# A vision tower with a mixture of experts on one core: the small steps of the attention stage in a new order

## The chip, the core and the metric

The kernel runs on one core of a Trainium2 chip. The core has TensorE (PE in the profile, with PEld for its weight loads), VectorE (DVE), ScalarE (ACT), GpSimd (POOL) and SyncE (SP, which here only issues DMAs). Each engine takes its own instructions strictly in the order in which they are written, and engines wait for each other with semaphores. The metric is the time of one execution on the device in microseconds (us).

## What is computed

16 images of 1024 patches, embedded in 64 dimensions; then an attention layer with 8 heads of 8 dimensions and a bias by column; then a mixture of 8 experts of which each token takes 2.

```python
h = tok(x)                                   # patches @ W + b + pos_embed
h = h + attn(layernorm(h), ...)
h = h + ffn(layernorm(h), ...)

# attn
q, k, v = (x @ W + b).reshape(B, N, H, hd)   # for q, k and v
scores = einsum('bihd,bjhd->bhij', q, k) / sqrt(hd) + col_bias
out = einsum('bhij,bjhd->bihd', softmax(scores), v) @ Wo + bo

# ffn
probs = softmax(tokens @ router_w.T)
rw, re = top_k(probs, 2); rw = rw / max(rw.sum(-1), 1e-12)
out = tokens
for e in range(8):
    h = gelu(tokens @ w1[e] + b1[e])
    out = out + combine[:, e] * (h @ w2[e] + b2[e])
```

## The kernel before

After a short first part (constants, the column bias, the preparation of the first images) the kernel has two stages: attention over the 16 images one after the other, and the experts over 64 units, four per image. The change touches the attention stage alone.

One image of attention is 32 **quads** (`QUADS`). A quad is two **blocks**, each a tile of 128x1024 scores in one of three PSUM buffers (`SCORE_BUFS`). In quad q TensorE issues four matmuls of scores (L1448, bf16), then a small step if one has its place there, then the eight passes of values of quad q - 2 (L1464, probabilities times v, accumulated in `o_acc` over eight quads). ScalarE takes the exp of each block (L1246), 64 per image. The scores of a block wait for the exp that last used its buffer; the values wait for the exps of their quad.

The small steps serve the neighbouring images. While image b is in attention, steps for the next image b + 1 run (`PREP`: qk0 and qk1 make the two halves of q and k, v makes v, sq the squares from which a bound on the scores comes), the embedding and normalisation of b + 2 (`LEAD`: embed, norm_t), and what follows attention for b - 1 (`POST`: out_proj, post_t, router, combine_t). `AUX_SLOTS` is a table written by hand: quad number to step and half. All steps share one PSUM bank, `aux`. A step waits (`aux_drained`) until VectorE has read what the step before left there, and VectorE waits (`aux_filled`) for the matmuls.

VectorE runs through the same 32 slots. A slot is only an order there: VectorE goes on as soon as its waits allow. In each slot it first does the evacuation that is due (`evacuate`, L1314 to L1319, slots 9, 17, 25, and 1 of the next image: it transposes `o_acc` out of PSUM and divides by the sum; the next values that write `o_acc` wait for its first instruction), then scale_tokens, shift_of and flag_of, lead_centre or normalise if the slot is theirs, then the drain of the step that ended in this quad, then centre_tokens, ranking (rank_experts, order_experts) or weigh_experts. The drain of qk1 is followed by `split_high` and `split_low`, which cut q and k into bf16 parts; SyncE stores these parts and loads them back as QA and KA for the next image, behind block 32 for the first half of the heads. `shift_of` needs a square root that GpSimd makes from the result of sq (L387). The exps of the router run on ScalarE behind block `ROUTER_EXP_BLOCK`. At slots 0 and 16 stands a fallback for large scores, whose branch isn't taken here, but for which TensorE waits until ScalarE has come to block 0 or 32.

Names in the rows: L481 is the drain of qk0 and qk1, L495 the reduction of sq, L563 and L565 scale_tokens, L575 the drain of out_proj, L581 of post_t, L584 and L585 of router, L597 to L615 ranking, L621 to L635 weigh_experts, L456 the drain of embed, L430 with `centred` lead_centre, L468 normalise, L486 the drain of v, L591 of combine_t. On TensorE L662 is qk, L686 out_proj, L681 sq, L672 post_t, L691 router, L650 embed, L666 v, L696 combine_t, L656 norm_t.

Of the kernel before, what the change touches and what calls it, by code (L numbers as in the profile page):

```python
# [12 lines left out]
NB = 16  # L13
# [33 lines left out]
EVAC_SLOTS = {8 * g + 7 + LAG: g for g in range(3)}  # L47
LAST_EVAC_SLOT = LAG - 1

AUX_SLOTS = {0: ("qk0", 0), 2: ("qk0", 1), 4: ("qk1", 0), 6: ("qk1", 1), 8: ("out_proj", 0), 10: ("out_proj", 1),  # L50
             12: ("sq", 0), 14: ("post_t", 0), 16: ("router", 0), 18: ("router", 1), 20: ("embed", 0),
             22: ("embed", 1), 24: ("v", 0), 26: ("v", 1), 28: ("combine_t", 0), 30: ("norm_t", 0)}
HALVED = ["qk0", "qk1", "out_proj", "router", "v", "embed"]
LEAD = ["embed", "norm_t"]
PREP = ["qk0", "qk1", "v", "sq"]
POST = ["out_proj", "post_t", "router", "combine_t"]
FIRST_STEPS = ["embed_0", "embed_1", "norm_t_0", "qk0", "qk1", "v", "sq", "norm_t_1"]
FIRST_DRAINS = ["embed_0", "embed_1", "qk0", "qk1", "v", "sq", "norm_t_1"]
CENTRE_SLOT, SCALE_SLOT, SHIFT_SLOT, LEAD_SLOT, NORM_SLOT = 10, 12, 14, 23, 26
ROUTER_EXP_BLOCK = 40  # L60
BUF_TURN = 38

PAIRS = NX // 2
# [5 lines left out]
CENTRE_UNIT, SCALE_UNIT = 4, 5  # L69
ROUTER_UNIT = 15  # L70
RANK_UNIT, ORDER_UNIT, WEIGH_UNIT = 16, 17, 18
COMBINE_SLOT, WEIGH_SLOT = 20, 25
Y_BUFS = 2
H_BUFS = 4
RQ_LIMIT, RQ_CLIP = 31.0, 32.0
# [15 lines left out]
def step_of(b, slot):  # L91

    if slot not in AUX_SLOTS:
        return None
    step, part = AUX_SLOTS[slot]
    image = b + (2 if step in LEAD else 1 if step in PREP else -1)
# [3 lines left out]
def is_last(step, part):  # L100
    return part == 1 or step not in HALVED
# [11 lines left out]
def aux_count(b, step):  # L113
    return aux_before(b) + aux_order(b).index(step) + 1
# [7 lines left out]
def attention(nc, pool, io, psum, scratch, out):  # L122
# [4 lines left out]
    with ctx:  # L127
# [173 lines left out]
        def later(b):  # L301

            return not (isinstance(b, int) and b == 0)

        def by_half(rows):
            return rows.rearrange("p (t c) d -> p t c d", t=2)

        def by_chunk(bank):
            return bank.rearrange("p (c t e) -> p t c e", t=2, e=D)

        def alone(eng):

            eng.sem_inc(stood_alone, 1)
# [88 lines left out]
        def vector_steps(v):  # L402

            def chain(sem, base, total):

                count = [0]

                def link(ins):
                    count[0] += 1
                    ins.then_inc(sem, 1)  # L410
                    v.wait_ge(sem, base + count[0])

                def close():
                    assert count[0] == total, (count[0], total)
                return link, close
# [55 lines left out]
            def prep_step(step, bp, filled, st, bank=aux, full=aux_filled, free=aux_drained, freed=None):  # L471

                freed = freed or filled
                if step == "qk0":
                    st["link"], st["close"] = chain(prep_chain, PREP_CHAIN * bp, PREP_CHAIN)
                link, close = st["link"], st["close"]
                if full is not None:
                    v.wait_ge(full, filled)
                if step in ("qk0", "qk1"):
                    n = int(step[-1])  # L480
                    v.tensor_scalar(qk[:, n * BANK:(n + 1) * BANK], bank, b_qk[:, 0:1], scale_qk[:, 0:1],  # L481
                                    ALU.add, ALU.mult).then_inc(free, 1)
                if step == "v":
                    if later(bp):
                        v.wait_ge(va_ready, 2 * bp)
                    v.tensor_tensor(by_half(v_new[:, :, :]), by_chunk(bank),  # L486
                                    b_v[:, :].unsqueeze(1).unsqueeze(1).broadcast_to([P, 2, NCH // 2, D]),
                                    ALU.add).then_inc(free, 1)
                elif step == "qk1":
                    v.wait_ge(free, freed)  # L490
                    split_high(bp, link)
                    if bp:
                        split_low(link)
                elif step == "sq":
                    v.reduce_max(sq_max[:, :], bank, AX.X).then_inc(free, 1)  # L495
                    v.wait_ge(free, freed)
                    alone(v)
                    square_bounds(link)
# [18 lines left out]
            def split_high(bp, link):  # L517
                if bp == 1:
                    v.wait_ge(first_stored[1], PARTS_STORES // 2)
                if bp > 1:  # L520
                    v.wait_ge(parts_stored, PARTS_STORES * (bp - 1))
                link(v.tensor_copy(qk_parts[:, 0, :], qk[:, :]))
                if bp:
                    link(v.tensor_tensor(qk_rest[:, :], qk[:, :], qk_parts[:, 0, :], ALU.subtract))
                v.tensor_tensor(squares[:, :], qk_parts[:, 0, :], qk_parts[:, 0, :],
                                ALU.mult).then_inc(squares_ready, 1)
                if not bp:
                    link(v.tensor_tensor(qk_rest[:, :], qk[:, :], qk_parts[:, 0, :], ALU.subtract))

            def split_low(link):  # L530
                link(v.tensor_copy(qk_parts[:, 1, :], qk_rest[:, :]))
                v.tensor_tensor(qk_parts[:, 2, :], qk_rest[:, :], qk_parts[:, 1, :],
                                ALU.subtract).then_inc(parts_ready, 1)

            def square_bounds(link):
                v.tensor_copy(sq_moved[:, 0:1], sq_max[SECOND:SECOND + H, :])
                v.tensor_copy(sq_moved[:, 1:2], sq_max[32:32 + H, :])
                link(v.tensor_copy(sq_moved[:, 2:3], sq_max[32 + SECOND:32 + SECOND + H, :]))
                v.tensor_tensor(q_sq_max[:, :], sq_max[0:H, :], sq_moved[:, 0:1], ALU.max)
                link(v.tensor_tensor(k_sq_max[:, :], sq_moved[:, 1:2], sq_moved[:, 2:3], ALU.max))  # L540
                v.tensor_tensor(rq2[:, :], q_sq_max[:, :], k_sq_max[:, :], ALU.mult).then_inc(rq2_ready, 1)
# [560 lines left out]
        with nc.Block() as block:  # L1102
# [136 lines left out]
            def _(act):  # L1239
# [27 lines left out]
                def body(b):  # L1267
                    act.wait_ge(flag_ready, b + 1)
                    flag = act.value_load(flags[0:1, ds(b, 1)], min_val=0, max_val=1)
                    for k in range(BLOCKS):  # L1270
                        if k % (BLOCKS // 2) == 0:
                            fallback(b, k // (BLOCKS // 2), flag)
                        exp_block(b, k)
                        if k == ROUTER_EXP_BLOCK and b:
                            router_exp(aux_count(b, "router"))
# [24 lines left out]

            @block.vector
            def _(v):
                chain, _, _, (lead_step, lead_centre, normalise), prep_step, (shift_of, flag_of), _ = vector_steps(v)
                post_step, centre_tokens, scale_tokens, rank_experts, order_experts, weigh_experts = vector_post(v)

                def evacuate(b, g):
# [46 lines left out]
                def body(b):  # L1353
                    v.wait_ge(flag_ready, b + 1)
                    flag = v.value_load(flags[0:1, ds(b, 1)], min_val=0, max_val=1)
                    st = {}
                    for slot in range(QUADS):
                        if slot % 16 == 0:
                            fallback(b, slot // 16, flag)
                        if slot in EVAC_SLOTS:  # L1360
                            evacuate(b, EVAC_SLOTS[slot])
                        if slot == SCALE_SLOT and b:
                            scale_tokens(b - 1, st)
                        if slot == SHIFT_SLOT and b + 1 < NB:
                            shift_of(b + 1, st)
                            flag_of(b + 1, st)
                        if slot == LEAD_SLOT and b + 2 < NB:
                            lead_centre(b + 2, st)
                        if slot == NORM_SLOT and b + 2 < NB:
                            normalise(b + 2)  # L1370
                        found = step_of(b, slot)
                        if found and is_last(found[0], found[1]):
                            step, _, image = found
                            if step in LEAD:
                                lead_step(step, image, aux_count(b, step), st)
                            elif step in PREP:
                                prep_step(step, image, aux_count(b, step), st)
                            else:
                                post_step(step, image, aux_count(b, step), st)
                        if slot == LAST_EVAC_SLOT and b:  # L1380
                            evacuate(b - 1, 3)
                        if slot == CENTRE_SLOT and b:
                            centre_tokens(b - 1, st)
                        if slot == COMBINE_SLOT and b:
                            rank_experts(b - 1, st)
                            order_experts(b - 1, st)
                        if slot == WEIGH_SLOT and b:
                            weigh_experts(b - 1, st)
# [18 lines left out]
                st = {}  # L1407
# [246 lines left out]
```

## Time and profile before

| | us |
|---|---|
| runs of the kernel | 1175.14, 1176.40, 1176.45 (median 1176.4) |
| profiled execution, its own time | 1174.37 |
| its span, first to last instruction | 1172.4 |
| TensorE busy | 1093.3 (93%) |
| ScalarE busy | 1029.6 (88%) |
| VectorE busy | 612.0 (52%) |
| GpSimd busy | 126.6 (11%) |

The granted clock of TensorE is 0.985 of full speed over the span and full from the second image of attention on. The first exp of attention starts at 47.6 us and the last at 1009.0; the rest is the experts. Busy shares are means over both stages. A row of the timeline gives the start, the duration, the engine and the line; "x4" means four instructions merged into one row, and the part in brackets is idle time of that engine ahead of it with the instruction that ended it. The start of a quad on TensorE is the start of the "x4" row of L1448.

### The profile page before, as it was taken

The page shows a single profiled execution, that of the slowest core. Times are in us where ns is not written, and L with a number is a line of the kernel's source. Part 1 is how long each engine was busy: PE and PEld are TensorE (multiplying, and loading weights), DVE is VectorE, ACT ScalarE, POOL GpSimd, SP SyncE. Part 2 cuts the span into 40 slices and gives each one's busy share as a digit, 9 for nine tenths or more (in the row PEclk, how much of TensorE's full clock was granted, in tenths as well). Part 3 has the DMA queues.
Part 4 walks back from the last instruction along what each step waited for, and adds up shares of the span by engine and source line. Part 5 has one row for each costly group of instructions (what it writes and reads, how often), then busy time and mean ns, then how long its engine had stood idle before and what let it go on. Part 6 is the DMA issues. An engine that isn't in the chain of part 4 may idle for free. (4 is left out here: it accounts for less than half of the span.)

```text
span 1172.4 us, 21673 instructions
## 1 busy us (share of the span) xinstructions
PE 1093.3 (93%) x7913; PEld 318.5 (27%) x7914; DVE 612.0 (52%) x1700; ACT 1029.6 (88%) x1127; POOL 126.6 (11%) x137
## 2 busy tenths in 40 slices
PE   3599999999999999999999999999999999899998
PEld 2122222222222222222222222222222222233332
DVE  8433555554545454555545454545454424467665
ACT  1399999999999999999999999999999999754553
POOL 3204010101001010101111110101010000000000
PEclk7699999999999999999999999999999999999999
DMA  2531313131222122323231322223131320022321
GB/s 53 123 84 41 92 42 92 43 89 43 82 46 73 49 76 51 83 51 83 52 83 47 87 48 61 74 56 78 40 86 33 92 61 10 14 61 71 84 73 50
DMA packets 62128, 75.06 MB, mean 64 GB/s; under 512 B 26220, under 2 KB 30572, under 8 KB 61996
## 3 DMA queue, kind: packets, MB, share of 16 engines
q1 hardware_dynamic: 59740, 73.03, 24.1%
q8 instruction: 79, 1.29, 0.5%
q14 instruction: 53, 0.43, 0.1%
q10 hardware_dynamic: 1776, 0.24, 0.1%
q0 software_dynamic: 480, 0.06, 0.1%
HBM read 36.70 MB, written 35.65 MB: 62 GB/s over the span
## 5 line engine op out<-in xcount | busy, mean ns | idle before, releaser
L1246 ACT ACTIVATE probs<-psum 128x1024 f32<-128x1024 f32 x1024 | 944.3, 1138 | 42.5 <-PE psum L1448 42.5
L1464 PE MATMUL psum<-probs,VA 128*32 128x512 f32 x4096 | 545.7, 605 | 1.1 <-ACT probs L1246 0.5
L1448 PE MATMUL psum<-QA,KA 54*128 54x512 bf16 x2048 | 326.2, 384 | 10.2 <-issue 3.1
L1448 PEld LDWEIGHTS psum<-QA,KA 54*128 54x128 bf16 x2048 | 74.4, 93 | 471.9 <-ACT probs L1246 436.9
L1314 DVE STREAM_TRANSPOSE oT<-psum 128x512 f32<-128x512 f32 x64 | 45.9, 717 | 218.6 <-PE psum L1464 218.6
L1464 PEld LDWEIGHTS psum<-probs,VA 128*32 128x32 f32 x4096 | 82.5, 108 | 147.5 <-issue 114.8
L1281 ACT ACTIVATE probs<-psum,b 128x1024 f32<-128x1024 f32 x64 | 67.8, 1110 | 53.4 <-PE psum L1517 53.4
L1395 DVE TENSOR_TENSOR probs<-probs,psum 128x1024 f32<-128x1024 f32 x64 | 78.2, 1221 | 51.3 <-PE psum L1527 31.1
L481 DVE TENSOR_SCALAR qk<-psum,b_qk,scale_qk 128x512 f32<-128x512 f32 x32 | 25.3, 793 | 85.3 <-PE psum L662 85.3
L1185 POOL TENSOR_TENSOR p_rstd<-p_ve,neg_half 128x8 f32<-128x8 f32 x16 | 32.3, 2021 | 310.5 <-DVE p_ve L427 310.5
L1517 PE MATMUL psum<-m_x,w 64*128 64x512 f32 x256 | 60.5, 591 | 1.5 <-ACT probs L1281 1.5
L1541 PE MATMUL psum<-probs,w 128*64 128x512 f32 x256 | 60.9, 598 | 0.0
L383 POOL TENSOR_TENSOR rstd<-ve,neg_half 128x8 f32<-128x8 f32 x16 | 31.5, 1970 | 266.5 <-DVE ve L427 266.5
L662 PE MATMUL psum<-xnT,w_qk 64*128 64x256 f32 x128 | 38.1, 398 | 0.8 <-ACT xnT L842 0.8
L392 POOL COPY VA<-v_new 128x256 f32<-128x256 f32 x32 | 12.7, 398 | 235.0 <-PE psum L1464 136.1
L462 DVE COPY xnT<-psum 128x512 f32<-128x512 f32 x15 | 10.4, 691 | 47.5 <-PE psum L656 47.5
L597 DVE TENSOR_REDUCE r_sum<-router_e 128x8 f32<-128x64 f32 x16 | 3.5, 220 | 54.0 <-ACT router_e L1251 54.0
L650 PE MATMUL psum<-w_tok,xT 128*128 128x128 f32 x128 | 23.2, 308 | 8.3 <-DMA tok_b<-in_tok_b 6.9
L1527 PE MATMUL psum<-m_cT,spread 64*128 64x512 bf16 x128 | 24.6, 382 | 6.2 <-DVE probs L1395 6.2
L1517 PEld LDWEIGHTS psum<-m_x,w 64*128 64x128 f32 x256 | 24.3, 188 | 19.3 <-issue 15.2
L1288 ACT ACTIVATE yT<-psum 128x512 f32<-128x512 f32 x16 | 9.6, 597 | 20.1 <-PE psum L1541 20.1
L1319 DVE TENSOR_TENSOR oT_norm<-oT,o_inv 128x128 f32<-128x128 f32 x64 | 24.7, 386 | 2.3
(171 smaller groups left out, 778.6 us busy)
## 6 DMA issues: line engine op xcount, KB each, us to landing
QA<-q_parts_d SPq DMA_DIRECT2D x64, 192.0 KB
KA<-k_parts_d SPq DMA_DIRECT2D x64, 192.0 KB
q_parts_d<-qk_parts SPq DMA_DIRECT2D x32, 192.0 KB, 2.4
k_parts_d<-qk_parts SPq DMA_DIRECT2D x32, 192.0 KB, 2.7
xT<-in_xT SPq DMA_DIRECT2D x16, 256.0 KB, 2.6
q_parts_d<-qk_parts SPq DMA_DIRECT2D x32, 128.0 KB, 2.6
k_parts_d<-qk_parts SPq DMA_DIRECT2D x32, 128.0 KB, 2.5
x_d<-x2T SPq DMA_DIRECT2D x16, 256.0 KB, 2.1
```

The source lines that it names most:

```text
L383: g.tensor_tensor(rstd[:, :], ve[:, :], neg_half[:, :], ALU.pow).then_inc(rstd_ready, 1)
L481: v.tensor_scalar(qk[:, n * BANK:(n + 1) * BANK], bank, b_qk[:, 0:1], scale_qk[:, 0:1], ALU.add, ALU.mult).then_inc(free, 1)
L662: last = pe.matmul(aux[:, cols], w_qk[rows, :, :].rearrange("k a e -> k (a e)"), xnT[rows, cols], start=True, stop=True)
L1185: g.tensor_tensor(p_rstd[:, :], p_ve[:, :], neg_half[:, :], ALU.pow).then_inc(p_rstd_ready, 1)
L1246: nc.scalar.activation(probs[:, k % PROB_BUFS, :], score_buf(buf_of(k)), ACT.Exp).then_inc(exped, 1)
L1281: nc.scalar.activation(act_h[:, u % H_BUFS, :], hid[u % 2], ACT.Gelu, bias=b1[:, u % PAIRS:u % PAIRS + 1]).then_inc(gelued, 1)
L1314: v.transpose(oT[:, :, :].rearrange("p j r -> p (j r)"), o_acc).then_inc(o_evacuated, 1)
L1395: v.tensor_tensor(gated[:, u % H_BUFS, :], act_h[:, u % H_BUFS, :], wgt, ALU.mult).then_inc(gated_ready, 1)
L1448: last = pe.matmul(score_buf(buf_of(k))[:, (g % 2) * BANK:(g % 2 + 1) * BANK], KA[rows_of(h, SCORE_ROWS), h // 2, jt * P:(jt + 1) * P], QA ...
L1464: last = pe.matmul(o_acc[32 * g:32 * g + 32, :], VA[:, jt, h, :], probs[:, k % PROB_BUFS, (g % 2) * BANK:(g % 2 + 1) * BANK], start=(jt == ...
L1517: last = pe.matmul(hid[u % 2][:, t * BANK:(t + 1) * BANK], w1[rows, m, :], m_x2[rows, b % 2, :], start=True, stop=True)
L1541: last = pe.matmul(ysum[D * t:D * (t + 1), :], w2[:, m, :], gated[:, u % H_BUFS, t * BANK:(t + 1) * BANK], start=False, stop=(m == PAIRS - 1))
```

## The change

`AUX_SLOTS` gets another order: out_proj goes from quads 8 and 10 to 4 and 6, qk1 from 4 and 6 to 8 and 10, post_t (the transposes of x) from 14 to 12, the router's halves from 16 and 18 to 14 and 16, sq from 12 to 18, the first half of embed from 20 to 19; all others keep their quads. On VectorE centre_tokens goes to slot 6, scale_tokens to 10, split_low gets a slot of its own (13), shift_of and flag_of go to 20, ranking to 19, weigh_experts to 22, normalise to 28. The router's exp on ScalarE goes from behind block 40 to behind block 36. No instruction is added or taken away.

```diff
...
-AUX_SLOTS = {0: ("qk0", 0), 2: ("qk0", 1), 4: ("qk1", 0), 6: ("qk1", 1), 8: ("out_proj", 0), 10: ("out_proj", 1),
...
+AUX_SLOTS = {0: ("qk0", 0), 2: ("qk0", 1), 4: ("out_proj", 0), 6: ("out_proj", 1), 8: ("qk1", 0), 10: ("qk1", 1),
...
-CENTRE_SLOT, SCALE_SLOT, SHIFT_SLOT, LEAD_SLOT, NORM_SLOT = 10, 12, 14, 23, 26
-ROUTER_EXP_BLOCK = 40
+CENTRE_SLOT, SCALE_SLOT, SPLIT_SLOT, SHIFT_SLOT, LEAD_SLOT, NORM_SLOT = 6, 10, 13, 20, 23, 28
+ROUTER_EXP_BLOCK = 36
...
-COMBINE_SLOT, WEIGH_SLOT = 20, 25
+COMBINE_SLOT, WEIGH_SLOT = 19, 22
...
                     split_high(bp, link)
-                    if bp:
-                        split_low(link)
...
+                        if slot == SPLIT_SLOT and b + 1 < NB:
+                            split_low(st["link"])
```

What stands in a row on each engine, at the places where the work moves. In these lines the operands stand behind the arrow, and line numbers of the changed kernel differ by one or two.

TensorE before, quads 12 to 14 of an image: sq, and two quads later the transposes of x.

```order
L1448 MATMUL psum<-QA,KA 128x512 x4
L681 MATMUL psum<-squares,sel_sq 32x512 x4
L1464 MATMUL psum<-probs,VA 32x512 x4
L1448 MATMUL psum<-QA,KA 128x512 x4
L1464 MATMUL psum<-probs,VA 32x512 x4
L1448 MATMUL psum<-QA,KA 128x512 x4
L672 MATMUL psum<-ident,x 128x128 x4
L1464 MATMUL psum<-probs,VA 32x512 x4
```

TensorE now, quads 10 to 12: the transposes of x come behind the second half of qk1.

```order
L1449 MATMUL psum<-QA,KA 128x512 x4
L660 MATMUL psum<-xnT,w_qk 128x256
L1465 MATMUL psum<-probs,VA 32x512 x4
L1449 MATMUL psum<-QA,KA 128x512 x4
L1465 MATMUL psum<-probs,VA 32x512 x4
L1449 MATMUL psum<-QA,KA 128x512 x4
L670 MATMUL psum<-ident,x 128x128 x4
L1465 MATMUL psum<-probs,VA 32x512 x4
```

TensorE now, quads 18 and 19: sq comes right ahead of the first half of embed, in neighbouring quads.

```order
L1449 MATMUL psum<-QA,KA 128x512 x4
L679 MATMUL psum<-squares,sel_sq 32x512 x4
L1465 MATMUL psum<-probs,VA 32x512 x4
L1449 MATMUL psum<-QA,KA 128x512 x4
L648 MATMUL psum<-w_tok,xT 128x128 x2
L1465 MATMUL psum<-probs,VA 32x512 x4
```

VectorE before, slots 12 to 14: scale_tokens, the reduction of sq, its bounds, shift and flags, and then the drain of the transposes of x.

```order
L563 TENSOR_TENSOR x<-p_centred,p_rstd 128x2x4x64
L565 TENSOR_TENSOR H_all<-h,x 128x512
L495 TENSOR_REDUCE sq_max<-psum 128x1
L536 COPY sq_moved<-sq_max 8x1
...
L541 TENSOR_TENSOR rq<-q_sq_max,k_sq_max 8x1
L506 TENSOR_SCALAR shift_row<-minus_ones,rq 8x1024
...
L514 TENSOR_SCALAR flags<-rq_top 1x1
L581 COPY x2T<-psum 128x512
```

VectorE now, slots 16 to 20: the evacuation stands ahead of the reduction of sq, and the ranking between its bounds and the shift.

```order
L583 TENSOR_TENSOR logits<-psum,logit_max 128x64
L1313 STREAM_TRANSPOSE oT<-psum 128x512
L1316 RECIPROCAL o_inv<-oT 128x16
L1318 TENSOR_TENSOR oT_norm<-oT,o_inv 128x16x8
L493 TENSOR_REDUCE sq_max<-psum 128x1
L534 COPY sq_moved<-sq_max 8x1
...
L595 TENSOR_REDUCE r_sum<-router_e 128x8
...
L613 TENSOR_REDUCE rank<-above 128x64
L504 TENSOR_SCALAR shift_row<-minus_ones,rq 8x1024
...
L512 TENSOR_SCALAR flags<-rq_top 1x1
```

VectorE before, slots 23 to 28: weigh_experts and normalise stand between the evacuation and the drain of v.

```order
L430 TENSOR_TENSOR centred<-H_all,mv 128x512
L1314 STREAM_TRANSPOSE oT<-psum 128x512
L1317 RECIPROCAL o_inv<-oT 128x16
L1319 TENSOR_TENSOR oT_norm<-oT,o_inv 128x16x8
L621 SCALAR_TENSOR_TENSOR chosen<-rank,rprob 128x64
...
L635 COPY comb_parts<-comb_parts 128x8x24
L468 TENSOR_TENSOR xn<-centred,rstd 128x2x4x64
L486 TENSOR_TENSOR v_new<-psum,b_v 128x512
L591 COPY cT<-psum 128x512
```

VectorE now, slots 22 to 28: weigh_experts stands ahead of lead_centre and the evacuation, and the drain of v right behind them, ahead of normalise.

```order
L456 TENSOR_TENSOR H_all<-psum,posb 128x512
L419 BN_STATS stats<-H_all 128x6 x8
L619 SCALAR_TENSOR_TENSOR chosen<-rank,rprob 128x64
...
L633 COPY comb_parts<-comb_parts 128x8x24
L425 BN_AGGR mv<-stats 128x2 x8
L427 TENSOR_SCALAR ve<-mv 128x8
L430 TENSOR_TENSOR centred<-H_all,mv 128x512
L1313 STREAM_TRANSPOSE oT<-psum 128x512
...
L1318 TENSOR_TENSOR oT_norm<-oT,o_inv 128x16x8
L486 TENSOR_TENSOR v_new<-psum,b_v 128x512
L468 TENSOR_TENSOR xn<-centred,rstd 128x2x4x64
L589 COPY cT<-psum 128x512
```

## Rows read from the trace of the kernel before

**Rows 1.** One line, ScalarE's exp: count, duration ns min/median/max, first and last start.
```profile
L1246 ACT ACTIVATE probs<-psum x1024: 1017/1124/1582, 47.6 to 1009.0; 128x1024 f32<-128x1024 f32 x171
```

**Rows 2.** ScalarE timeline, one image; columns: start, duration, engine, line, tiles, count, idle before.
```profile
497.99 10.19 ACT L1246 ACTIVATE probs<-psum 128x1024 f32<-128x1024 f32 x11 [0.55 <-PE psum L1448]
...
508.10 15.82 ACT L1246 ACTIVATE probs<-psum 128x1024 f32<-128x1024 f32 x17
...
524.65 33.10 ACT L1246 ACTIVATE probs<-psum 128x1024 f32<-128x1024 f32 x36 [0.73 <-PE psum L1448]
558.30 10.19 ACT L1246 ACTIVATE probs<-psum 128x1024 f32<-128x1024 f32 x11 [0.55 <-PE psum L1448]
```

**Rows 3.** Who waited for whom, whole span; columns: total us, times, longest.
```profile
PE psum L672 <- DVE sq_max L495: 12.4, 14, 1.0
...
PE psum L696 <- DVE v_new L486: 14.0, 14, 1.0
...
PEld psum L1448 <- ACTq L1265: 26.0, 31, 0.8
```

**Rows 4.** Timeline around the first stall, quads 14 and 15, PE and DVE.
```profile
493.84 0.69 DVE L563 TENSOR_TENSOR x<-p_centred,p_rstd 128x512 f32<-128x512 f32 x1 [1.61 <-POOL p_rstd L1185]
...
494.24 0.91 PE L1448 MATMUL psum<-QA,KA 54*128 54x512 bf16 x4
...
495.18 0.68 DVE L495 TENSOR_REDUCE sq_max<-psum 128x1 f32<-128x512 f32 x1
...
496.01 0.63 PE L672 MATMUL psum<-ident,x 128*128 128x128 f32 x4 [0.86 <-DVE sq_max L495]
...
497.56 0.61 PE L1448 MATMUL psum<-QA,KA 54*128 54x512 bf16 x4
...
497.69 0.47 DVE L506 TENSOR_SCALAR shift_row<-minus_ones,rq 8x1024 bf16<-8x1024 bf16 x1 [0.80 <-POOL rq L387]
...
498.58 0.69 DVE L581 COPY x2T<-psum 128x512 f32<-128x512 f32 x1
```

**Rows 5.** Timeline around the second stall, quads 26 to 30, DVE and PE.
```profile
517.77 0.72 DVE L1314 STREAM_TRANSPOSE oT<-psum 128x512 f32<-128x512 f32 x1 [1.64 <-PE psum L1464]
...
519.14 0.22 DVE L621 SCALAR_TENSOR_TENSOR chosen<-rank,rprob 128x64 f32<-128x64 f32 x1
...
521.24 0.61 PE L1448 MATMUL psum<-QA,KA 54*128 54x512 bf16 x4
...
521.55 0.68 DVE L468 TENSOR_TENSOR xn<-centred,rstd 128x512 f32<-128x512 f32 x1
522.15 0.68 DVE L486 TENSOR_TENSOR v_new<-psum,b_v 128x512 f32<-128x512 f32 x1
...
522.89 0.40 PE L696 MATMUL psum<-ident_bf,comb_parts 128*128 128x128 bf16 x4 [1.04 <-DVE v_new L486]
...
524.22 0.60 PE L1448 MATMUL psum<-QA,KA 54*128 54x512 bf16 x4
...
525.75 0.61 PE L1448 MATMUL psum<-QA,KA 54*128 54x512 bf16 x4
```

**Rows 6.** Timeline, steps that the change moves, DVE and PE, same image.
```profile
472.59 0.60 PE L1448 MATMUL psum<-QA,KA 54*128 54x512 bf16 x4
...
474.62 0.61 PE L1448 MATMUL psum<-QA,KA 54*128 54x512 bf16 x4
...
480.95 0.81 DVE L481 TENSOR_SCALAR qk<-psum,b_qk,scale_qk 128x512 f32<-128x512 f32 x1 [4.86 <-PE psum L662]
...
508.35 0.22 DVE L597 TENSOR_REDUCE r_sum<-router_e 128x8 f32<-128x64 f32 x1 [3.59 <-ACT router_e L1251]
...
510.11 0.61 PE L1448 MATMUL psum<-QA,KA 54*128 54x512 bf16 x4
...
512.29 0.61 PE L1448 MATMUL psum<-QA,KA 54*128 54x512 bf16 x4
...
515.45 0.69 DVE L430 TENSOR_TENSOR centred<-H_all,mv 128x512 f32<-128x512 f32 x1
```

More of the change, by code:

```diff
@@ L48 @@
 LAST_EVAC_SLOT = LAG - 1
-AUX_SLOTS = {0: ("qk0", 0), 2: ("qk0", 1), 4: ("qk1", 0), 6: ("qk1", 1), 8: ("out_proj", 0), 10: ("out_proj", 1),
-             12: ("sq", 0), 14: ("post_t", 0), 16: ("router", 0), 18: ("router", 1), 20: ("embed", 0),
-             22: ("embed", 1), 24: ("v", 0), 26: ("v", 1), 28: ("combine_t", 0), 30: ("norm_t", 0)}
+AUX_SLOTS = {0: ("qk0", 0), 2: ("qk0", 1), 4: ("out_proj", 0), 6: ("out_proj", 1), 8: ("qk1", 0), 10: ("qk1", 1),
+             12: ("post_t", 0), 14: ("router", 0), 16: ("router", 1), 18: ("sq", 0), 19: ("embed", 0), 22: ("embed", 1),
+             24: ("v", 0), 26: ("v", 1), 28: ("combine_t", 0), 30: ("norm_t", 0)}
 HALVED = ["qk0", "qk1", "out_proj", "router", "v", "embed"]
@@ L1302, in _ @@
             def _(v):
-                chain, _, _, (lead_step, lead_centre, normalise), prep_step, (shift_of, flag_of), _ = vector_steps(v)
+                chain, _, _, (lead_step, lead_centre, normalise), prep_step, (shift_of, flag_of), rest = vector_steps(v)
+                split_low = rest[2]
                 post_step, centre_tokens, scale_tokens, rank_experts, order_experts, weigh_experts = vector_post(v)
```

## The prediction, made before the changed kernel was run

> **What bounds the kernel now.** The page's busy shares, which I read first, do not decide it: TensorE and ScalarE both look nearly full, over two stages of different kinds. So I read ScalarE's own timeline over one image of the attention stage. ScalarE runs 64 exps of 128x1024 per image. One stretch of 36 of them takes 33.10 us from first start to last end, and the shortest of all exps is 1.02 us, so one exp costs (33.10 - 1.02) / 35 = **0.917 us** when nothing is late [rows 1, 2]. 64 of them are 58.67 us. The image's period is 558.30 - 497.99 = 60.31 us [rows 2]. Of the 1.64 us between them, about 0.16 is the small exp of the router, which sits before 508.10: the 17 exps behind it need 15.59 and end at 523.92, 15.74 after the end of the 11 exps before it. The other **1.48 us** are two idle times with "PE psum L1448" as releaser: 0.55 us ahead of block 30 and 0.73 us ahead of block 58 [rows 2]. Since neighbouring exps overlap by 1.02 - 0.92 = 0.10 us, each costs 0.10 more than its idle time: 0.65 and 0.83.
>
> So ScalarE bounds the attention stage, except in two places per image where the scores of TensorE come late. Who made them late? Two waits stand out by their counts: TensorE's transposes of x (L672) waited for sq_max on VectorE 14 times, 12.4 us in all, and its transposes of the expert weights (L696) for v_new 14 times, 14.0 us in all, at most 1.0 us each [rows 3]. Fourteen is the number of images that have both a next image to prepare and one before to finish (images 1 to 14).
>
> In rows 4 to 6 one reads "quad starts" (the x4 rows of L1448). At the first stall quad 14 starts at 494.24, VectorE reduces sq only at 495.18 to 495.86, because scale_tokens stood before it, and the transposes, which write the same PSUM bank, start at 496.01, having waited 0.86. Quad 15 begins at 497.56 instead of about 1.2 earlier, and block 30's exp follows 0.43 after that [rows 2, 4]. At the second, weigh_experts starts at 519.14, xn at 521.55 and v_new at 522.15, so the aux bank is free only at 522.83, while quad 28 had begun at 521.24; the wait is 1.04 and quad 29 starts at 524.22, 0.43 before block 58's exp [rows 2, 5].
>
> **How much room TensorE has.** A quad without a small step lasts 525.75 - 524.22 = 1.53 us [rows 5], one with half of embed 512.29 - 510.11 = 2.18 [rows 6], one with half of qk0 and an evacuation by VectorE, which the values must await, 474.62 - 472.59 = 2.03 [rows 6], the combine transposes without their wait 524.22 - 521.24 - 1.04 = 1.94 [rows 5]. ScalarE takes 2 x 0.917 = 1.83 per quad. I call lead the time by which a quad starts before it would delay an exp; that point is 0.43 + 0.10 = 0.53 before the end of the exp ahead. A quad without a step adds 0.30 to the lead, one with a step takes 0.11 (combine), 0.20 (qk) or at most 0.35 (all other). Check on before: the second stall. The 17 exps end at 508.10 + 15.82 = 523.92, less 0.53 is 523.39, quad 29 starts at 524.22: lead -0.83, which is the loss read above. The whole of TensorE's image is 60.31 less the two waits with what they made wait, 0.86 + 1.04, so at most 58.4, below ScalarE's 58.83: with the waits gone ScalarE can set the pace, with little to spare.
>
> **The change, part by part.**
>
> Step 1: out_proj goes to quads 4 and 6, qk1 to 8 and 10. All counts stay. out_proj needs qk0's drain and the last evacuation of the image before, both queued at quad 2. That evacuation takes 519.14 - 517.77 = 1.37 [rows 5], plus a transpose of about 0.7, then the drain of 0.81 [rows 6], together 3.0 from 0.2 into quad 2; out_proj is due 2.03 + 1.53 + 0.54 = 4.1 into it (0.54 being the scores ahead of a step). Hidden, cover 0.9.
>
> Step 2: the transposes of x (post_t) go to quad 12, behind qk1 instead of sq. VectorE from 0.2 into quad 10: evacuation 1.37, scale_tokens 495.18 - 493.84 = 1.34 or a little more [rows 4], qk1's drain 0.81, and about 0.12 to TensorE: bank free 3.9 into quad 10. TensorE arrives at 2.03 + 1.53 + 0.54 = 4.1. The wait of 0.86 goes, cover 0.2. This frees **0.65 us**.
>
> Step 3: split_low (some 1.9 us, two of VectorE's 128x1024 operations) moves behind the drain of post_t, to slot 13. Its 12 stores on SP start some 7 quads later; behind them on SP stand the store of x2, the loads of QA and KA for the next image, which wait for block 32 anyway, and the row of shifts, which is now made at slot 20. The next image starts 12 quads, 22 us, after that slot, and a chain of some 20 issues fits in; then come the load of x, wanted in the next image's quad 19, and the store of the combine weights. Cost nothing; if the stores took over 20 us more, the next image would start late. The router's halves at 14 and 16 wait for x2T, which comes after split_high, about 3 us behind the qk1 drain; quad 14's step is due 3.7 after quad 12's. Cost nothing.
>
> Step 4: sq goes to quad 18. VectorE is then at the evacuation of slot 17 for 1.37 from 0.2 into the quad, reduces sq in 0.68 and frees the bank 2.4 into it. The first half of embed now stands in quad 19 and is due 2.03 + 0.54 = 2.57 into quad 18. Cover 0.2: the **tightest place**. If gone, each 0.1 beyond the lead costs 0.1 per image. Quad 18 itself grows: sq alone would be under 2.03, but the evacuation holds the values; I take 2.03.
>
> Step 5: ranking (slot 19), shift (20), embed and weighing (22), then lead_centre (23), then the evacuation of slot 25, due 0.2 into quad 26. On VectorE, from 1.6 into quad 18: the sq reduction and bounds, shift and flags are 498.58 - 495.18 = 3.40, less the 0.80 wait for POOL that ranking now covers, 2.6 [rows 4]; ranking, embed and centring 516.14 - 508.35 = 7.8 [rows 6]; weighing 521.55 - 519.14 = 2.4 [rows 5]. It ends 14.5 after quad 18's start. Quad 26 starts 8 quads after, 8 x 1.83 + 0.14 = 14.8, and its evacuation is due at 15.0. Cover about 0.5. Behind it v is drained and xn made, before quad 28's transposes are due 3.7 + 0.5 after quad 26. The wait of 1.04 goes: **0.83 us**.
>
> Leads in the new order. After quad 16, TensorE cannot start before ScalarE has come to block 32 (the ACTq row, 31 times) [rows 3]; before, the lead there was 0.30 (zero after the stall, one free quad). From 0.30 at quad 0: 0.10 after it, then 0.20, 0.15, 0.10, 0.20, 0.30, 0.25, 0.20 after quads 2 to 14. From 0.30 at 16: -0.05 at 17, 0.30 at 18, with the router's exp 0.24 at 19, -0.11 at 20; then 0.60 at 22, 0.25, 0.20, 0.15 after 22, 24, 26, and 0.3 at the end. So the worst is 0.16 per image. But ScalarE's starts run ahead of its ends when it is not made to wait, and then quad 16 may start with 0.5, and nothing is lost. The bounds are 0 and 0.16 x 14 = 2.2 us; I take 0, as no stall resets ScalarE at quad 15.
>
> **Sum.** 14 x (0.65 + 0.83) = 20.7 us. The first image, the last one and the feed-forward stage keep their order of costs. The profiled execution took 1174.4 us and becomes 1153.7; the runs' median is 1176.4, 2.0 above it, and becomes **1155.7**.
>
> **A rule that speaks against it.** The trace gives 0.917 per exp over 36 in a row, and 1.02 for the shortest alone [rows 1, 2]. The Trainium skill, "ScalarE: Activation LUTs", section "What ACT_TABLE_LOAD costs", gives 186 ns plus 0.833 ns per element, with back-to-back activations overlapping by about 93 ns: an estimate of 946 ns for 1024. By it ScalarE would need 60.5 + 0.16 us per image, more than the measured period, and there would be nothing to win: 1176. The trace disagrees by 0.03 per exp.
>
> **Rivals.**
> (a) Forecast: both stalls vanish, 1153 to 1158.
> (b) One cover is gone. At quad 19 or before the evacuation of quad 26 VectorE is late by 0.3 to 0.8 us more than I count, and the lead of 0.1 to 0.5 swallows part. Loss 0.2 to 0.7 per image, 3 to 10 us: 1158 to 1166. For it: covers of 0.2 in steps 2 and 4. Against: durations on VectorE repeat from image to image.
> (c) No gain: ScalarE is saturated in a way that gives the idle back, for instance each exp stretched to 0.94 once it is fed without pause. 64 x 0.94 = 60.2, or 1.4 more than ScalarE needs here, which eats the 1.48: about 1175. This is where the rule above would lead. Against: 36 exps in a row run at 0.917 [rows 2].
> (d) Slower: VectorE's unbroken run of 13 us between quads 18 and 26. If ranking can't start when sq is done, because the router's exp comes after block 36 and is itself late, everything to the evacuation slides. From 0.5 + 0.5 us of slide TensorE's values wait and ScalarE stalls; from 2.5 us it costs more than the 1.48 gained. At 3.5 us it is 1.0 x 14 = +14, so 1190. Against: the logits are made 2 quads ahead of block 36, as before they were of block 40.
>
> **Chances.** (a) 0.74, (b) 0.16, (c) 0.04, (d) 0.06. A measurement tells about 0.2%, 2.4 us, from no change: faster 0.90, same 0.04, slower 0.06. The range holds (a) with its 2.2 us and the runs' own 1.3 us of spread, and the larger part of (b): 1152.5 to 1163.
>
> **What would show it.** Right: the waits of L670 (transposes of x) for sq_max and of the combine transposes for v_new are gone; ScalarE's timeline has no idle in an image, and the period is 58.8 us. Step 4 wrong: embed's matmuls wait for sq_max in quad 19. Step 5 wrong: values in quad 26 wait for oT's transpose. Step 2 wrong: the transposes of x wait for qk. Rival (c): exps of over 0.92 us without idle between them.

## The result and the profile after

| | before | after |
|---|---|---|
| median of the runs | 1175.77 us | 1154.60 us (1154.36 to 1155.46) |
| ratio after to before | | 0.9823, 95% interval 0.9806 to 0.9840 |
| span of the profiled execution | 1172.4 us | 1152.3 us |

The change makes the kernel 21 us faster, against 1155.7 us predicted. The profiled execution took 1154.4, against 1153.7 predicted. With the same two views as in [rows 2, 3], ScalarE's timeline of the changed kernel (start, duration, line, tiles, count) reads:

```profile
469.00 26.12 ACT L1244 ACTIVATE probs<-psum 128x1024 f32<-128x1024 f32 x28
494.70 0.55 ACT L1249 ACTIVATE router_e<-logits 128x64 f32<-128x64 f32 x1
494.85 59.08 ACT L1244 ACTIVATE probs<-psum 128x1024 f32<-128x1024 f32 x64
553.50 0.55 ACT L1249 ACTIVATE router_e<-logits 128x64 f32<-128x64 f32 x1
```

There is no idle time left in brackets. 64 exps go from 494.85 to the next router exp without one, and the period is 553.50 - 494.70 = 58.80 us, where [rows 2] had 60.31. 13 of the 14 full images had two stalls, image 14 one and a small one. From the starts of the exps in the two traces: images 1 to 14 took 843.9 us before and 823.2 after, 20.8 less; the first image 0.4 less, the last 0.2 more, the time ahead of the first exp 0.7 more. From the start of the last exp to the end it is 163.3 before and 163.5 after. With this the parts add up to the difference of the spans, 20.0. The 0.7 ahead of the first exp is no effect of the change: that exp starts anywhere between 47.5 and 48.5 us in the runs below.

The page's groups for ScalarE's exp, before and after (line, tiles, count, busy us, mean ns, idle before it, releaser):

```profile
L1246 ACT ACTIVATE probs<-psum 128x1024 f32<-128x1024 f32 x1024 | 944.3, 1138 | 42.5 <-PE psum L1448 42.5
```

```profile
L1244 ACT ACTIVATE probs<-psum 128x1024 f32<-128x1024 f32 x1024 | 940.9, 1249 | 25.7 <-PE psum L1449 25.7
```

Of this idle time 23.8 and 24.5 us lie ahead of the very first exp (the longest single wait in the list of waits), so inside the stage it falls from 18.7 to 1.2 (the 1.2 is one wait in the first image, which both kernels have). With the 0.10 us of overlap that each of the 27 stalls also destroys, these are 20.2 of the 20.8 us. The mean duration rises from 1138 to 1249 ns although each exp costs the same, 0.917 us between ends. I read this as waiting behind the exp ahead that is recorded inside the duration. Durations of single exps say nothing here; distances between ends do.

Now the covers of the critical steps, that is the time between VectorE's release of what TensorE waits for and TensorE's use of it. Quad 12, the transposes of x behind the drain of qk1 (before: [rows 4]):

```profile
481.31 0.80 DVE L481 TENSOR_SCALAR qk<-psum,b_qk,scale_qk 128x512 f32<-128x512 f32 x1
...
482.02 0.72 PE L1449 MATMUL psum<-QA,KA 54*128 54x512 bf16 x4
...
482.66 0.66 PE L670 MATMUL psum<-ident,x 128*128 128x128 f32 x4
```

The bank is free at 482.11 and used at 482.66, with no wait. Behind the first stall stood one more wait, which the prediction shows in its rows and does not reason with. In [rows 4] VectorE sat idle for 1.61 us before scale_tokens, until GpSimd had made `p_rstd` from the result of centre_tokens. The lists of waits, before and after:

```profile
DVE x L563 <- POOL p_rstd L1185: 24.4, 16, 1.6
```

```profile
DVE x L561 <- POOL p_rstd L1183: 0.3, 1, 0.3
```

Before, two slots lay between the two steps, and TensorE waited 0.86 us behind them; now there are four, and GpSimd's result is there in time. Without the 1.61 us the reduction of sq would have ended at about 494.25, ahead of the transposes, which were due at 495.15. So this idle time alone accounts for the first stall. No run moves scale_tokens by itself, so that is worked out and not shown. Quads 18 and 19, sq and embed:

```profile
493.08 0.66 PE L1449 MATMUL psum<-QA,KA 54*128 54x512 bf16 x4
...
494.65 0.68 DVE L493 TENSOR_REDUCE sq_max<-psum 128x1 f32<-128x512 f32 x1
...
495.18 0.61 PE L1449 MATMUL psum<-QA,KA 54*128 54x512 bf16 x4
...
495.71 0.71 PE L648 MATMUL psum<-w_tok,xT 128*128 128x128 f32 x4
```

sq is read by 495.33, embed's matmuls come 0.53 into quad 19, where they are due, at 495.71: 0.38 later. Quads 26 and 28 (before: [rows 5]):

```profile
508.01 0.61 PE L1449 MATMUL psum<-QA,KA 54*128 54x512 bf16 x4
508.25 0.72 DVE L1313 STREAM_TRANSPOSE oT<-psum 128x512 f32<-128x512 f32 x1 [0.42 <-PE psum L1465]
...
509.62 0.68 DVE L486 TENSOR_TENSOR v_new<-psum,b_v 128x512 f32<-128x512 f32 x1
...
512.26 0.40 PE L694 MATMUL psum<-ident_bf,comb_parts 128*128 128x128 bf16 x4
```

VectorE is idle for 0.42 us before the evacuation of quad 26, so its long run (from the reduction of sq on, see step 5 of the prediction) ended that much before its time, and v is drained at 510.30, 2 us before the transposes of the expert weights.

### The profile page after: what moved, and what is told of

The parts are those of the page before. It is cut to its first block and busy times, and to the rows that moved or that the text cites. A ratio compares the mean times of both kernels' runs of the same rounds, so it can differ in the third digit from the quotient of the medians.

```text
span 1152.3 us, 21645 instructions
## 1 busy us (share of the span) xinstructions
PE 1100.7 (96%) x7913; PEld 326.2 (28%) x7914; DVE 610.2 (53%) x1700; ACT 1026.2 (89%) x1127; POOL 130.2 (11%) x137
## 5 line engine op out<-in xcount | busy, mean ns | idle before, releaser
L1244 ACT ACTIVATE probs<-psum 128x1024 f32<-128x1024 f32 x1024 | 940.9, 1249 | 25.7 <-PE psum L1449 25.7
L1449 PE MATMUL psum<-QA,KA 54*128 54x512 bf16 x2048 | 331.8, 385 | 8.4 <-issue 3.6
L1449 PEld LDWEIGHTS psum<-QA,KA 54*128 54x128 bf16 x2048 | 82.2, 93 | 484.5 <-ACT probs L1244 446.5
L573 DVE TENSOR_TENSOR h<-psum,H_all 128x512 f32<-128x512 f32 x16 | 11.1, 692 | 80.9 <-PE psum L684 80.9
L387 POOL TENSOR_TENSOR rq<-rq,half 8x1 f32<-8x1 f32 x16 | 8.7, 546 | 307.1 <-DVE rq L539 307.1
L392 POOL COPY VA<-v_new 128x256 f32<-128x256 f32 x32 | 16.4, 513 | 194.1 <-PE psum L1465 175.5
L582 DVE TENSOR_REDUCE logit_max<-psum 128x8 f32<-128x64 f32 x16 | 3.6, 224 | 53.6 <-PE psum L689 53.6
L1518 PEld LDWEIGHTS psum<-m_x,w 64*128 64x128 f32 x256 | 24.3, 188 | 19.2 <-issue 15.2
```

Source lines behind the costliest of these rows:

```text
L1244: nc.scalar.activation(probs[:, k % PROB_BUFS, :], score_buf(buf_of(k)), ACT.Exp).then_inc(exped, 1)
L1449: last = pe.matmul(score_buf(buf_of(k))[:, (g % 2) * BANK:(g % 2 + 1) * BANK], KA[rows_of(h, SCORE_ROWS), h // 2, jt * P:(jt + 1) * P], QA ...
L1518: last = pe.matmul(hid[u % 2][:, t * BANK:(t + 1) * BANK], w1[rows, m, :], m_x2[rows, b % 2, :], start=True, stop=True)
```

## The experiments

All times below are medians of four runs or more; the kernel before had medians of 1175.1 to 1175.4 beside them, and the ratios are to it. "Lead" is used as in the prediction. It was computed in each trace from the end of the exp ahead and the start of the quad.

**1. The first half of the change alone.** weigh_experts and normalise go back to their slots.

```diff
-CENTRE_SLOT, SCALE_SLOT, SPLIT_SLOT, SHIFT_SLOT, LEAD_SLOT, NORM_SLOT = 6, 10, 13, 20, 23, 28
+CENTRE_SLOT, SCALE_SLOT, SPLIT_SLOT, SHIFT_SLOT, LEAD_SLOT, NORM_SLOT = 6, 10, 13, 20, 23, 26
-COMBINE_SLOT, WEIGH_SLOT = 19, 22
+COMBINE_SLOT, WEIGH_SLOT = 19, 25
```

> The changed kernel with weigh_experts back at slot 25 and normalise back at 26, all else as changed (the first half of the change alone). Theory (VectorE's order makes the aux bank late for the transposes of combine): v's drain ends 3.0 us later than now (weighing 2.4, xn 0.6), the transposes in quad 28 wait 1.1 us; the lead of TensorE there is 0.41 us, so the loss is 0.73 per image, 9.7 us over 14 images: 1164 us, with one idle time of ScalarE per image, ahead of block 58, and none ahead of block 30. Rival (the quads of TensorE's steps alone made the gain): no change, 1154.6.

Measured 1164.16 us, ratio 0.9909 (0.9892 to 0.9925). ScalarE's timeline:

```profile
498.77 19.66 ACT L1244 ACTIVATE probs<-psum 128x1024 f32<-128x1024 f32 x21
519.05 39.52 ACT L1244 ACTIVATE probs<-psum 128x1024 f32<-128x1024 f32 x43 [0.63 <-PE psum L1449]
```

One stall per image, 21 exps after the router's (block 58), of 0.63 + 0.10 = 0.73 us, as expected to the hundredth; the lead at quad 29 is -0.73. So the first half removes the first stall and 11 us, and the second half is worth the other 9.6. Apart from split_low (experiment 4) the parts of the first half were not run one by one.

**2. The second half alone, in the kernel before.**

```diff
-CENTRE_SLOT, SCALE_SLOT, SHIFT_SLOT, LEAD_SLOT, NORM_SLOT = 10, 12, 14, 23, 26
+CENTRE_SLOT, SCALE_SLOT, SHIFT_SLOT, LEAD_SLOT, NORM_SLOT = 10, 12, 14, 23, 28
-COMBINE_SLOT, WEIGH_SLOT = 20, 25
+COMBINE_SLOT, WEIGH_SLOT = 20, 22
```

> The kernel before with weigh_experts at slot 22 and normalise at 28 (the second half of the change alone). Theory: the wait of 1.04 us for v_new goes, but ranking still ends as late as before, so weighing pushes the evacuation of slot 25 0.8 us past its time and the values of quad 26 wait 0.67; TensorE has no lead there (-0.01), so ScalarE loses 0.68 in quad 27 instead of 0.84 in quad 29: 1174, 2 us under before. The releaser of the new wait is VectorE's transpose of oT. Rival (each half is worth its own stall): 11 us under before, 1165.

Measured 1174.59 us, ratio 0.9993 (0.9983 to 1.0002): nothing that can be told from no change. The timeline of quad 26, VectorE, TensorE and ScalarE:

```profile
518.51 0.61 PE L1448 MATMUL psum<-QA,KA 54*128 54x512 bf16 x4
...
518.85 0.68 DVE L430 TENSOR_TENSOR centred<-H_all,mv 128x512 f32<-128x512 f32 x1
...
519.57 0.72 DVE L1314 STREAM_TRANSPOSE oT<-psum 128x512 f32<-128x512 f32 x1
...
520.43 1.07 PE L1464 MATMUL psum<-probs,VA 128*32 128x512 f32 x8 [0.67 <-ACT probs L1246]
...
521.86 2.85 ACT L1246 ACTIVATE probs<-psum 128x1024 f32<-128x1024 f32 x3 [0.65 <-PE psum L1448]
```

The transpose of the evacuation, due 0.24 into the quad at 518.75, starts at 519.57 behind lead_centre, and the values wait 0.67. The row names ScalarE as releaser, but the two exps of quad 24, which these values read, had ended by 517.55; the values start 0.14 after the transpose's end at 520.29. The stall moves from block 58 to block 54 and keeps most of its size (0.65 + 0.10 against 0.83). Together the two parts of the second half need the first half, which ends ranking earlier; experiment 3 takes them apart.

**3. Only normalise later, in the kernel before.** NORM_SLOT 26 becomes 28.

> The kernel before with normalise at slot 28 instead of 26, one constant. Theory: v's drain comes 0.6 us earlier, the wait for v_new falls from 1.04 to 0.44 us and the loss from 0.84 to 0.24 per image: 0.6 x 13 = 7.8 us under before, 1168. Rival (the stall at block 58 is made by the length of the transposes or the late weighing, not by the bank): no change, 1176.

Measured 1167.59 us, ratio 0.9936 (0.9920 to 0.9953): 7.6 us for one constant. The waits of TensorE's transposes, in the kernel of this run:

```profile
PE psum L672 <- DVE sq_max L495: 12.4, 14, 1.0
...
PE psum L696 <- DVE v_new L486: 6.2, 14, 0.4
```

The wait for v_new falls from 14.0 us in all [rows 3] to 6.2, the one for sq_max stays, and the loss at quad 29 falls from 0.84 to 0.24. This shows the bank as the cause of the second stall: the length of the transposes was not touched. It also says what failed in experiment 2: normalise alone wins 7.6 us in the old kernel, and weighing earlier on top of it loses 7.0 of them again (1174.59 against 1167.59).

**4. split_low back behind split_high.**

```diff
-                        if slot == SPLIT_SLOT and b + 1 < NB:
-                            split_low(st["link"])
...
                                 prep_step(step, image, aux_count(b, step), st)
+                                if slot == SPLIT_SLOT:
+                                    split_low(st["link"])
```

with SPLIT_SLOT at 10, the slot of qk1's drain.

> The changed kernel with split_low back right behind split_high, in slot 10, ahead of the drain of post_t. Theory: the drain of post_t ends 1.95 us later; it has 0.8 us to spare now, so the router's matmuls in quad 14 wait 1.15 us; the lead there is 0.56 and the step takes 0.25, so 0.85 to 0.95 us lost per image, 12 to 13 us: 1167. Rival (a slot of its own for split_low does nothing, since it is the same work on the same engine): 1154.6.

Measured 1165.55 us, ratio 0.9920 (0.9903 to 0.9936).

```profile
490.63 0.62 PE L1449 MATMUL psum<-QA,KA 54*128 54x512 bf16 x4
491.46 0.68 DVE L579 COPY x2T<-psum 128x512 f32<-128x512 f32 x1
...
492.19 0.52 PEld L689 LDWEIGHTS psum<-w_router,x2T 128*128 128x128 f32 x4 [1.25 <-DVE x2T L579]
492.20 0.62 PE L689 MATMUL psum<-w_router,x2T 128*128 128x16 f32 x4 [0.95 <-DVE x2T L579]
...
493.74 0.60 PE L1449 MATMUL psum<-QA,KA 54*128 54x512 bf16 x4
...
494.17 1.02 ACT L1244 ACTIVATE probs<-psum 128x1024 f32<-128x1024 f32 x1 [0.62 <-PE psum L1449]
```

The router's matmuls, due at 491.2, start at 492.20, 1.0 late instead of the 1.15 expected, and 0.73 plus a later 0.05 is lost per image. That is 11 us, where 12 to 13 were expected. Half of what the change gains depends on the one line that splits split_low off.

**5. ScalarE lighter.** All exps but the first eight take 992 of 1024 columns.

```diff
-                    nc.scalar.activation(probs[:, k % PROB_BUFS, :], score_buf(buf_of(k)),
+                    w = 2 * BANK if b == 0 and k < PROB_BUFS else 2 * BANK - 32
+                    nc.scalar.activation(probs[:, k % PROB_BUFS, 0:w], score_buf(buf_of(k))[:, 0:w],
```

> The changed kernel with the exps over 992 of the 1024 columns (all but the first eight of the first image); the last 32 columns of each block keep old values, so part of the softmax is left out. Theory (ScalarE bounds each image at 58.80 us, TensorE needs 58.0): an exp falls by 0.027 us to 0.890, 64 by 1.7, and TensorE takes over: a period of 58.0 to 58.4, 6 to 12 us less, 1143 to 1149. Rival 1 (TensorE bounds already): no change, 1154.6. Rival 2 (TensorE has much room): 1.7 x 16 = 27 less, 1127.

Measured 1139.38 us, ratio 0.9691 (0.9675 to 0.9708), below the expected range of 1143 to 1149. Its timeline:

```profile
488.43 0.27 ACT L1250 ACTIVATE router_e<-logits 128x64 f32<-128x64 f32 x1
488.58 2.79 ACT L1245 ACTIVATE probs<-psum 128x992 f32<-128x992 f32 x3
491.53 54.99 ACT L1245 ACTIVATE probs<-psum 128x992 f32<-128x992 f32 x61 [0.16 <-PE psum L1450]
546.39 0.27 ACT L1250 ACTIVATE router_e<-logits 128x64 f32<-128x64 f32 x1
```

The period is 546.39 - 488.43 = 57.96. Between the ends of exps that nothing delays the trace has 0.890, so ScalarE needs 64 x 0.890 + 0.13 = 57.09, and the other 0.87 per image are stalls again, many and small. So TensorE bounds here, at 57.96: its quads follow each other at the durations given in the prediction, 1.53 us without a step. The expected period was right at its lower end (58.0); the time was missed since I counted 14 images alike, while ScalarE is lighter in all 16. By the starts of the exps images 1 to 14 gain 12.3 us (0.84 each, more in image 14), the first image 0.9 and the last 1.7; the spans differ by 14.8 and the medians by 15.2.

**6. TensorE lighter.** Half of out_proj is left out in all images but one.

```diff
                     pe.wait_ge(on_ready, GROUPS * (n + 1))
+                    if n and part == 0:
+                        chunks = []
                     for c in chunks:
```

> The changed kernel without the two matmuls of out_proj's first half in all images but one; half of h1 is then made of what the bank held, so that part of the result is left out. TensorE has 0.64 us less in quad 4 of each image. Theory (ScalarE bounds): no change, period 58.80, 1154.6. Rival (TensorE bounds): 0.64 x 14 = 9 less, 1145.6.

Measured 1154.62 us, ratio 0.9819 (0.9803 to 0.9836), against 1154.60. TensorE's 0.64 us per image are worth nothing: ScalarE sets the pace of the changed kernel.

**7. weigh_experts alone back at slot 25.**

> The changed kernel with weigh_experts alone back at slot 25; normalise stays at 28. Theory: v's drain is 2.4 us later, the transposes of quad 28 wait 0.51 us, the lead of 0.41 with 0.03 taken by the step leaves -0.13: 0.13 x 14 = 1.8 us more, 1156.4, at the edge of what can be measured, but the period in the trace is 58.93 against 58.80. Rival (a wait costs its whole length): 0.5 x 14 = 7 more, 1161.7.

Measured 1156.24 us, ratio 0.9835 (0.9818 to 0.9851). The period in the trace is 58.93, the lead at quad 29 -0.13. By the medians alone 1.6 us could not be told from nothing; the trace confirms the expectation. A wait of TensorE of about 0.5 us costs 0.13, because the lead pays for the rest.

**8. The tightest place, measured.** sq is read twice, the first time into a scratch column.

```diff
+                    if bp:
+                        v.reduce_max(fb_max[:, 0:1], bank, AX.X)
                     v.reduce_max(sq_max[:, :], bank, AX.X).then_inc(free, 1)
```

> The changed kernel with one more reduction of the same sq bank (0.68 us, into a scratch column) ahead of the real one, in slot 18. It measures the cover of the tightest place. Theory: the drain of sq ends 0.73 us later, it has 0.26 to spare, so the first half of embed in quad 19 waits 0.47; the lead after quad 19 is 0.12, so 0.35 per image is lost, 14 x 0.35 = 5: 1159.5. Rival 1 (VectorE is off the path): no change. Rival 2 (the delay runs on to the evacuation of quad 26 too): 0.73 x 14 = 10 more, 1165.

Measured 1156.17 us, ratio 0.9835 (0.9819 to 0.9852), a period of 58.96 and 0.16 lost per image, not the 0.35 expected.

```profile
494.93 0.68 DVE L494 TENSOR_REDUCE fb_max<-psum 128x1 f32<-128x512 f32 x1
...
495.46 0.60 PE L1451 MATMUL psum<-QA,KA 54*128 54x512 bf16 x4
495.53 0.68 DVE L495 TENSOR_REDUCE sq_max<-psum 128x1 f32<-128x512 f32 x1
...
496.27 0.52 PEld L650 LDWEIGHTS psum<-w_tok,xT 128*128 128x128 f32 x4 [0.70 <-DVE sq_max L495]
496.27 0.71 PE L650 MATMUL psum<-w_tok,xT 128*128 128x128 f32 x4 [0.20 <-DVE sq_max L495]
```

Two reductions that don't wait for each other start 0.60 apart, not 0.73, and TensorE starts 0.06 after VectorE's end (496.21), not 0.12. The matmuls are 0.28 late (due at 495.99). So the cover in this place is 0.60 - 0.28 = 0.32 us. My theory held in kind (a delay there costs what cover and lead don't pay, and doesn't run on); its size was half.

**9. Embed's first half at quad 20.** `19: ("embed", 0)` becomes `20: ("embed", 0)`.

> The changed kernel with the first half of embed back in quad 20, so that it no longer stands right behind sq. Theory: quad 20 gets a lead of 0.76 and loses 0.35 to 0.5 in the step; after the second half in 22 the leads are about 0.15, 0.10 and 0.05 at 23, 25 and 27, none negative, so nothing is lost and nothing gained: period 58.80, 1154.6. The move to 19 was not needed. Rival (the steps must be spread by one quad): leads below zero at 25 and 27, 0.05 to 0.1 per image, 1 us more.

Measured 1156.50 us, ratio 0.9839 (0.9823 to 0.9856), a period of 58.95, 0.15 lost per image. My theory was wrong. Quad 20 has a lead of 0.33, not 0.76:

```profile
496.31 0.60 PE L1449 MATMUL psum<-QA,KA 54*128 54x512 bf16 x4
...
498.27 0.61 PE L1449 MATMUL psum<-QA,KA 54*128 54x512 bf16 x4 [0.37 <-ACT probs L1244]
```

Quad 20 waits 0.37 for an exp. The table `buf_of` of the three score buffers makes a turn at block `BUF_TURN` = 38, so that the buffers fit again in the next image: block 38 takes the buffer of 36 and block 40 that of 38, two blocks back instead of three. The scores of quad 20 therefore can't start until exp 38 has ended; they start some 0.05 us later. Exp 39, the one ahead of quad 20, ends 0.917 after exp 38, so the lead is 0.917 - 0.05 - 0.53, or 0.33.

**10. Both cuts of 5 and 6.**

> Both cuts at once, exps over 992 columns and out_proj without its first half in all images but one, so part of the softmax and of h1 is left out. With short exps alone the period was 57.96; alone the second cut did nothing. Theory (TensorE bounds once the exps are shorter): now the second cut counts, up to 0.64 per image but not below ScalarE's 64 x 0.890 + 0.13 = 57.1: period 57.3 to 57.7, that is 4 to 10 us under the 1139.4 of the short exps alone: 1130 to 1135. Rival (0.890 is not all that ScalarE needs and it still bounds): 1139.

Measured 1135.24 us, ratio 0.9659 (0.9643 to 0.9675): 4.1 us under experiment 5, just above the expected 1130 to 1135; the period of 57.66 is within its range. The cut that did nothing in experiment 6 counts here, which shows TensorE as the bound of experiment 5. It counts only 0.30 of its 0.64. TensorE's timeline, quads 5 and 6:

```profile
461.43 0.71 PE L1452 MATMUL psum<-QA,KA 54*128 54x512 bf16 x4
...
463.08 0.85 PE L1452 MATMUL psum<-QA,KA 54*128 54x512 bf16 x4
```

Scores that need not wait take 0.61. Right behind the step that was left out TensorE comes too early for a score buffer and waits 0.1 and 0.24, so over half of the 0.64 is lost on the spot: with three buffers a lead beyond some 0.6 us is not kept. The rest keeps the quads up to 13 from being late; the losses from quad 15 on (at quad 20 a lead of -0.26) are as in experiment 5.

**11. Embed at quad 20, and the turn of the buffers at block 30.**

```diff
-BUF_TURN = 38
+BUF_TURN = 30
```

> The changed kernel with embed's first half back in quad 20 and the turn of the three score buffers at block 30 instead of 38. At the turn, two blocks (38 and 40 so far, now 30 and 32) take the buffer of the block two before, not three, so their quads can't start before that exp has ended, and the lead is held to 0.33. Theory: this hold, at quad 20 just ahead of embed, is what cost 0.147 us per image in the run with embed at 20; at quads 15 and 16 it finds leads of 0.29 and 0.59, cuts the second to 0.33, and the leads then stay at or above zero (about 0.0 at 17, 0.2 at 21, 0.1 to 0.2 at 23 to 27): period 58.80 to 58.85, 1154.6 to 1155.3, against 1156.5. Rival (the density of embed and v in 20, 22, 24 and 26 alone made the loss): 58.95 as with embed at 20 alone, 1156.5.

Measured 1154.29 us, ratio 0.9822 (0.9806 to 0.9839). The period is 58.82 and the leads at quads 21, 23, 25 and 27 are 0.20, 0.15, 0.11 and 0.07. So it was the turn, not the density of the steps, that cost experiment 9 its 0.15. The changed kernel has its step in quad 19, and comes out of it with a lead of 0.12, less than the 0.33 that the turn allows, so that the turn takes nothing. The version is as fast as the changed one, not faster.

## Why the prediction was right

**What bounds.** Right. ScalarE's 0.917 per exp and 58.83 per image became the period of 58.80; experiments 5, 6 and 10 show that the changed kernel follows ScalarE down until TensorE's 57.96. The prediction gave at most 58.4 for TensorE.

**The terms.** The two stalls were 0.65 and 0.83; experiment 1 separates them and gives 0.73 for the second, not 0.83, where the first is gone: TensorE has more lead at quad 28 then (0.41 against 0.30), and pays more of the wait. In sum 20.7 predicted, 20.8 measured in images 1 to 14, and 20.0 over the profiled executions. That is partly luck: image 14 had only 0.10 of the second stall, because it has no image after the next to normalise. Made up for it: 0.01 more per second stall, 0.015 in each image at quad 27, 0.13 more in image 1, and first stalls that were 0.12 longer in images 4 and 14. The first stall was put down to scale_tokens ahead of the reduction of sq; that is right, but the 1.61 us that VectorE waited for GpSimd's `p_rstd` in front of it was left out of the reasoning.

**Covers.** Step 1: out_proj doesn't wait. Step 2: 0.55 between the bank's release and its use, or 0.49 without the 0.06 that the signal takes by experiment 8, against 0.2 predicted. I had let TensorE arrive by its own durations only; in the trace it waits for score buffers in quads 10 and 12 (their scores last 0.69 and 0.72 instead of 0.61) and arrives 0.2 later than I counted; VectorE is 0.1 earlier. Step 4: 0.32 by experiment 8, 0.2 predicted. Step 5: 0.42, about 0.5 predicted. All hold. Of step 3 "cost nothing" was right but says too little: experiment 4 shows that split_low can't stand earlier, it would cost 11 us.

**Leads.** The worst case, 0.16 per image, didn't come: quad 16 starts with 0.59, the case that I took. After quad 16 the smallest leads are 0.12, at quads 20 and 27. The recurrence missed one hold, the turn of the buffers at quads 19 and 20, which is visible before as well: there quad 19, without a step, lasts 506.40 - 504.79 = 1.61 instead of 1.53. It had no effect on the result, since the step in quad 19 leaves less than 0.33 anyway, but it made the expectation of experiment 9 wrong.

**Rivals.** (b) is refuted by the trace after: TensorE's matmuls have no wait in quads 19 and 26 of images 1 to 14. (c) did not come: 0.917 between ends is kept over 64 exps without a pause. (64 x (0.94 - 0.917) is 1.5 and not the 1.4 of the prediction, so (c) would have given 1176.) By the figures of the Trainium skill, "ScalarE: Activation LUTs", section "What ACT_TABLE_LOAD costs", the estimate for 1024 columns is 946 ns, which no stretch here shows. The 0.833 ns per element of that section agrees with the traces: experiment 5 took 32 columns away and an exp fell from 0.917 to 0.890 between ends, 0.83 ns per column. So what the estimate has 0.03 us too large here is the part that does not depend on the columns. (d) did not come, and experiments 2 and 3 show its mechanism in the old surroundings: weighing ahead of the evacuation, with ranking late, costs 7.0 us.

## What to carry to other kernels

When two engines are both near full, follow the time between their ends quad by quad: a small step costs only what the lead of the feeding engine doesn't pay, so one badly placed wait of 1 us costs 0.8 and another of 0.5 costs 0.13. A bank shared by many small steps is freed in the order of the draining engine's program; put the drain that the feeder waits for ahead of work that nobody waits for (7.6 us for one constant in experiment 3). And look whether moves depend on each other: earlier weighing cost 7.0 us while ranking was late (experiment 2 against 3) and was worth 1.6 after ranking had been moved (experiment 7), while the later normalise was worth 7.6 in the old kernel and 7.9 in the new one (experiment 1 against 7).

## What was not expected of the hardware

Starts of exps on ScalarE come 0.903 us apart while their ends are 0.917 apart, when the input is there; the recorded duration grows by 0.013 per exp, from 1.02 up to 1.58 us. In the trace before, input that comes late first shortens the recorded duration, and costs time only when it has fallen back to 1.02. So a distance of 0.98 between starts, 0.08 more than usual, mostly cost nothing there. It is also why idle time of ScalarE understates a stall by 0.10.
